# A selective scan laid out as 32 channels times 4 states, in a block with attention, feed-forward and routed low-rank layers

## What is computed

```python
dt = softplus(x_dbc[..., :R] @ dt_w + dt_b)
Bm, Cm = x_dbc[..., R:R + N], x_dbc[..., R + N:]          # N = 16 states
def step(h, inp):                                          # over the 512 tokens
    h = exp(dtt[..., None] * A) * h + (xt * dtt)[..., None] * Bt[:, None, :]
    y = einsum('bn,bdn->bd', Ct, h)                        # sum over the states
    return h, y
y = (y + x_c * D_param) * silu(z)
ssm_out = y @ ssm_out_w
```

## Time and profile before

| | |
|---|---|
| median of the runs | 5182.9 us (5181.59 to 5184.66, 3 runs) |
| span of the profiled execution | 5180.5 us |
| mean granted TensorE clock | 0.992 |
| PE busy | 4966.1 us, 96% |
| DVE busy | 4756.7 us, 92% |
| POOL busy | 4631.1 us, 89% |
| ACT busy | 4017.9 us, 78% |
| DMA | 812.29 MB, 157 GB/s |

### The profile page before, as it was taken

How to read it: one execution, slowest core, us unless ns; L and a number is a source line. 1 busy time by engine, 2 the same in 40 slices (tenths; PEclk the granted TensorE clock), 3 DMA queues, 4 the chain that set the end, 5 groups by cost and what they waited for, 6 DMA issues and landing times.

```text
span 5180.5 us, 94636 instructions
## 1 busy us (share of the span) xinstructions
PE 4966.1 (96%) x32312; PEld 3448.9 (67%) x32312; DVE 4756.7 (92%) x7342; ACT 4017.9 (78%) x6417; POOL 4631.1 (89%) x2933
## 2 busy tenths in 40 slices
PE   5899999999999999999999999999999999999998
PEld 2566666667666667666676666676666676666766
DVE  5999999999999999999999999999999999999985
ACT  4787887877877877877878878778778778787774
POOL 5899999999999999999999999999999999999984
PEclk7999999999999999999999999999999999999999
DMA  5455555555555555555555555555555545555552
GB/s 155 155 156 153 157 166 160 162 157 152 163 166 161 162 155 151 171 166 159 154 153 159 168 162 161 155 153 162 164 164 157 156 152 168 162 164 153 155 153 68
DMA packets 522032, 812.29 MB, mean 157 GB/s; under 512 B 80992, under 2 KB 227848, under 8 KB 521552
## 3 DMA queue, kind: packets, MB, share of 16 engines
q1 hardware_dynamic: 516784, 805.96, 51.2%
q10 hardware_dynamic: 4768, 0.28, 0.1%
HBM read 716.57 MB, written 88.38 MB: 155 GB/s over the span
## 4 chain that ended last, share of the span: by engine, by line
PE 72%; DVE 10%; issue 8%; POOL 5%; DMA 3%; SPq 1%; ACT 1%; DVEq 0%; POOLq 0%; ACTq 0%
PE pY L1083 12%; PE pM L1232 8%; PE pM L1241 8%; PE pM L1125 4%; PE pM L1219 4%; PE pM L1159 4%; PE pM L1172 4%; DVE pD L1466 4%; PE pM L1092 4%; PE pM L1105 3%; PE pM L1192 3%; POOL state L631 2%; PE pM L1133 2%; PE pM L1216 2%; PE pM L1140 2%
## 5 line engine op out<-in xcount | busy, mean ns | idle before, releaser
L631 POOL TENSOR_TENSOR state<-scan_in,bc 128x1024 f32<-128x1024 f32 x1024 | 2406.5, 2363 | 148.6 <-PE pY L1083 136.8
L788 ACT ACTIVATE pD<-scan_in,A 128x512 f32<-128x512 f32 x2048 | 1404.3, 690 | 400.8 <-DVE state L1474 315.3
L1466 DVE TENSOR_TENSOR_SCAN pD<-pD,state 128x512 f32<-128x512 f32 x1280 | 1545.1, 1219 | 68.9 <-ACT pD L788 67.6
L1083 PE MATMUL pY<-ident,state 128*128 128x128 f32 x8192 | 1152.6, 275 | 33.6 <-POOL state L619 26.6
L619 POOL TENSOR_TENSOR state<-state,bc 128x512 f32<-128x512 f32 x768 | 969.9, 1274 | 153.8 <-DVE state L1466 153.7
L1083 PEld LDWEIGHTS pY<-ident,state 128*128 128x128 f32 x8192 | 907.4, 142 | 269.2 <-issue 107.9
L1514 DVE TENSOR_REDUCE mx<-pM 128x1 f32<-128x512 f32 (+3 forms) x1408 | 859.9, 630 | 156.9 <-PE pM L1174 149.3
L1466 DVE TENSOR_TENSOR_SCAN state<-pD,state 128x512 f32<-128x512 f32 x768 | 916.3, 1210 | 57.3 <-ACT pD L788 57.2
L889 ACT ACTIVATE region<-pM 128x512 f32<-128x512 f32 (+1 forms) x1408 | 741.7, 559 | 179.6 <-PE pM L1194 157.0
L1474 DVE TENSOR_TENSOR state<-pD,bc 128x512 f32<-128x512 f32 x1280 | 862.0, 680 | 11.0
L1172 PE MATMUL pM<-region 96*128 96x512 bf16 (+3 forms) x2048 | 521.1, 301 | 25.8 <-DVE region L1531 11.1
(11 more groups left out here) (215 smaller groups left out, 8123.9 us busy)
## 6 DMA issues: line engine op xcount, KB each, us to landing
bc<-bc_d SPq DMA_DIRECT2D x2048, 256.0 KB, 3.9
region<-qk_d SPq DMA_DIRECT2D x640, 128.0 KB, 3.6
qk_d<-qkp SPq DMA_DIRECT2D x64, 384.0 KB, 3.4
qk_d<-ht SPq DMA_DIRECT2D x64, 384.0 KB, 5.1
xt<-in_x_dram SPq DMA_DIRECT2D x32, 512.0 KB, 5.4
hres_d<-xt SPq DMA_DIRECT2D x32, 512.0 KB, 4.4
region<-qk_d SPq DMA_DIRECT2D x256, 64.0 KB, 3.1
x<-hres_d SPq DMA_DIRECT2D x32, 512.0 KB, 5.2
```

The source lines that it names most:

```text
L631: nc.gpsimd.tensor_tensor(state[:, at_:at_ + JP], us[:, parity(b), k // N * JP:(k // N + 1) * JP, :], bc[:, k % BC_SLOTS, 0, :].unsqueeze( ...
L788: act.activation(pD[DECAY_BANK[e]][:], dts[:, parity(b), j], ACT.Exp, scale=A[:, j, n:n + 1]).then_inc(a_ok.sem, 1)
L1083: ins = pe.matmul(y_part(t, e % JP), state[:, e % RING, t * P:(t + 1) * P], ident[:], is_transpose=True, start=False, stop=(e % PASS >= PA ...
L1466: v.tensor_tensor_scan(h if e in POOL_C else decay, decay, h, 0.0, ALU.mult, ALU.add)\
```

## The change

The scans are laid out anew. A tile of 128 partitions now holds 32 channels times 4 states. There are 16 blocks of 32 channels; a pair of blocks and a group of 4 states is one unit, so there are again 32 units of two scans.

- dt and u are written to DRAM (`dtu_d`, two stores a turn), and read back 16 times a turn so that each row of 32 channels lands on four groups of partitions (`rep`, two slots). B and C need 8 loads a turn in place of 64, and stay for the whole turn.
- Every scan writes to `state` in SBUF. The C multiply is one operation of 128 x 1024 per unit, in place, on DVE for 20 units and on POOL for 12 (`k % 8` in 2, 5, 7).
- The states are added by PE: for each scan one product of the constant `sel` (128 x 32) with 512 columns of `state`, into the 32 rows of `pY` that belong to the block. The result has channels on the partitions, so `yt` (PE and ACT) is gone; `z` is computed with channels on the partitions too. The `D_param` term is a product with a diagonal matrix, so `ud` is gone.
- dt and u have one copy, `dtu`, where there were two. `nrm`, `ax`, `axT` and `gT` lie in it.
- All five orders and the bank places are new.

```diff
-UNITS = N * J // JP
+HALVES = J // JP
+CH = 32
+REP = P // CH
+SG = N // REP
+BLOCKS = DI // CH
+PAIRS = BLOCKS // JP
+UNITS = PAIRS * SG
 SCANS = UNITS * JP
-PASSES = J // JP
-PASS = SCANS // PASSES
+PASS = UNITS // J
 RING = 8
-BC_SLOTS = 4
-POOL_C = [e for e in range(SCANS) if e // JP % 4 == 3 or e % (4 * JP) == 2 * JP - 1]
+SLOTS = 2
+POOL_C = [k for k in range(UNITS) if k % 8 in (2, 5, 7)]
...
-        scan_in = sb("scan_in", [P, 2, 2, J, L])
-        dts, us = scan_in[:, :, 0], scan_in[:, :, 1]
+        dtu = sb("dtu", [P, J, 2, L])
+        dts, us = dtu[:, :, 0], dtu[:, :, 1]
+        rep = sb("rep", [P, SLOTS, JP, 2, L])
-        bc = sb("bc", [P, BC_SLOTS, 2, L])
+        bc = sb("bc", [P, 2, SG, L])
...
+            def spread(b, c):
+                if c % (PAIRS // HALVES) == 0:
+                    b.wait(sp, dtu_out[c * HALVES // PAIRS])
...
+                for i in range(JP):
+                    first = (c * JP + i) * CH
+                    src = dtu_d[b.index, first:first + CH].rearrange("d a t -> d (a t)")
+                    sp.dma_start(rep[:, c % SLOTS, i].rearrange("p a t -> p (a t)"),
+                                 src.unsqueeze(0).broadcast_to([REP, CH, 2 * L])).then_inc(rep_in[c % SLOTS].sem, 16)
...
+            def times_c(b, k):
+                at_, g = k * JP % RING, k % SG
+                b.wait(pool, s_ok, (k + 1) * JP)
+                b.wait(pool, bc_in[1][g])
+                nc.gpsimd.tensor_tensor(state[:, at_:at_ + JP], state[:, at_:at_ + JP],
+                                        bc[:, 1, g, :].unsqueeze(1).broadcast_to([P, JP, L]), ALU.mult).then_inc(pp_ok.sem, 1)
...
-                nc.gpsimd.tensor_tensor(state[:, at_:at_ + JP], us[:, parity(b), k // N * JP:(k // N + 1) * JP, :],
-                                        bc[:, k % BC_SLOTS, 0, :].unsqueeze(1).broadcast_to([P, JP, L]),
-                                        ALU.mult).then_inc(b_ok.sem, 1)
+                b.wait(pool, bc_in[0][g])
+                b.wait(pool, *rep_landed(c))
+                nc.gpsimd.tensor_tensor(state[:, at_:at_ + JP], rep[:, c % SLOTS, :, 1, :],
+                                        bc[:, 0, g, :].unsqueeze(1).broadcast_to([P, JP, L]), ALU.mult).then_inc(b_ok.sem, 1)
...
-                    b.wait(act, *decay_read_after(e - 1 - scanned))
+                    b.wait(act, s_ok, e + 1 - DECAYS)
...
-            def add(b, e):
-                b.wait(pe, *product_after(e))
-                for t in range(TB):
-                    ins = pe.matmul(y_part(t, e % JP), state[:, e % RING, t * P:(t + 1) * P],
-                                    ident[:], is_transpose=True, start=False,
-                                    stop=(e % PASS >= PASS - JP), skip_group_check=True)
+            def add(b, k):
+                j = k // PASS
+                b.wait(pe, *product_after(k))
+                for i in range(JP):
+                    rows = slice((k // SG % 2 * JP + i) * CH, (k // SG % 2 * JP + i + 1) * CH)
+                    ins = pe.matmul(pY[j % len(pY)][rows], sel[:], state[:, k * JP % RING + i], start=False,
+                                    stop=(k % SG == SG - 1), skip_group_check=True)
...
-                decay, h = pD[DECAY_BANK[e]][:], state[:, e % RING]
-                v.tensor_tensor_scan(h if e in POOL_C else decay, decay, h, 0.0, ALU.mult, ALU.add)\
-                 .then_inc(s_ok.sem, 1)
+                h = state[:, e % RING]
+                v.tensor_tensor_scan(h, pD[e % DECAYS][:], h, 0.0, ALU.mult, ALU.add).then_inc(s_ok.sem, 1)
...
-                v.tensor_tensor(state[:, e % RING], pD[DECAY_BANK[e]][:], bc[:, slot, 1, :], ALU.mult)\
-                 .then_inc(p_ok.sem, 1)
+            def times_c(b, k):
+                at_, g = k * JP % RING, k % SG
+                b.wait(dve, s_ok, (k + 1) * JP)
+                b.wait(dve, bc_in[1][g])
+                v.tensor_tensor(state[:, at_:at_ + JP], state[:, at_:at_ + JP],
+                                bc[:, 1, g, :].unsqueeze(1).broadcast_to([P, JP, L]), ALU.mult).then_inc(p_ok.sem, 1)
...
     "SP": """
+        qk3 xp -rp7 +load ld0 bb0 du0 bb1 -mt3 rp0 ld2 bb2 bb3 cc0 rp1 cc1 cc2 cc3 du1 ld1 mt0 rp2 rp3 +l1a -xr rp4
+        mt1 +qk0 rp5 x1p +qk1 rp6 ld3 -put +qk2 mt2
     """,
     "POOL": """
+        -fill27 -fill28 u0 -fill29 -pc26 u1 +l0s -fill30 -fill31 -pc29 fill0 fill1 -pc31 fill2 +l0a fill3 +l0b fill4
...
```

More of the change, by code:

```diff
@@ L462, in _ @@
                          d["lora_A"][:, k * P:(k + 1) * P, :].rearrange("e p r -> p e r"), w_late)
+            with nc.allow_non_contiguous_dma(reason="state indices go to partitions, once"):
+                for m in range(REP):
+                    for g in range(SG):
+                        n = g * REP + m
+                        load(A[m * CH:(m + 1) * CH, :, g:g + 1],
+                             d["A_log"][:, n:n + 1].rearrange("(c d) o -> d c o", d=CH), a_in)
+            assert n_loads.pop(a_in.name) == REP * SG
             assert n_loads == {"w_first": FIRST_LOADS, "w_loaded": N_LOADS - ACT_LOADS, "w_late": LATE_LOADS}, n_loads
@@ new lines, in step @@
+            def step(name, b):
+                if name[:2] in ("bb", "cc"):
+                    bc_rows(b, int(name[0] == "c"), int(name[2:]))
+                elif name[:2] == "rp":
+                    spread(b, int(name[2:]))
+                elif name[:2] == "du":
+                    h = int(name[2])
+                    b.wait(sp, u_ok, h + 1)
+                    rows = slice(h * JP * P, (h + 1) * JP * P)
+                    sp.dma_start(dtu_d[b.index, rows].rearrange("(j p) a t -> p j a t", p=P), dtu[:, h * JP:(h + 1) * JP])\
+                      .then_inc(dtu_out[h].sem, 16)
@@ L567, in _ @@
                 sp.wait_ge(qk_out[n].sem, 32 * B)
-            sp.wait_ge(bc_out.sem, 16 * PASSES * B)
+            sp.wait_ge(bc_out.sem, 16 * B)
+            for h in range(HALVES):
+                sp.wait_ge(dtu_out[h].sem, 16 * B)
         @block.gpsimd
@@ L801, in step @@
                 elif name == "l2a":
-                    normalise(b, 2, nrm(b), x1, n2)
+                    if not is_last(b):
+                        for h in range(HALVES):
+                            b.next().wait(act, dtu_out[h])
+                    normalise(b, 2, nrm, x1, n2)
                 elif name == "l3a":
-                    normalise(b, 3, nrm(b), xr, n3)
-                elif name == "ud":
-                    b.wait(act, u_ok)
-                    for j in range(J):
-                        act.activation(xc[:, j], xc[:, j], ACT.Copy, scale=D_par[:, j:j + 1]).then_inc(xd_ok.sem, 1)
+                    normalise(b, 3, nrm, xr, n3)
                 elif name[:2] == "xt":
@@ L1459, in _ @@
             dve.wait_ge(w_loaded, 16 * N_LOADS)
+            for j in range(J):
+                link(v.tensor_scalar(diag[:, j], ident[:], D_par[:, j:j + 1], None, ALU.mult))
+            assert count[0] == DIAG_READY
             def scan(b, e):
@@ L1664 @@
              + [(1, [0, 1]), (1, [2, 3]), (0, [0, 1, 2, 3])])
-N_LOADS = 24
+N_LOADS = 23
 ACT_LOADS = 17
```

364 lines of the change are left out of this document (162 added, 202 removed).

## The result

The changed kernel takes 7047.6 us (median of 4 runs, 7031.1 to 7057.9) against 5183.5 for the kernel before, a ratio of 1.359 with a 95% interval of 1.357 to 1.362. The sign came as forecast, the size did not: the forecast was 5700 us, in a range that ended at 5960.

What follows compares the result with a forecast made beforehand. It took PE to bound the kernel before, at 96% busy, with DVE and POOL close behind. After the change, contention makes a turn 173.2 us: 330.5 + 31 x 173.2 = 5700 us, range 5170 to 5960.

Steps and rivals of the forecast that it cites:

- the contention: DVE's two-SBUF multiplies and POOL's operations hold each other up: POOL 24.6 us, DVE 20 us more a turn.
- POOL and DVE were to be busy 95% or more: Sign in the profile after the change: waits from contention count as busy, with PE about 85%.
- where I put 1.0: DVE's mean wait per two-SBUF multiply for the rest of a running POOL operation: 1.0 us, 20 us a turn.
- my 0.96: PE's new adds: 0.96 us for each pair of products running side by side, 30.7 us a turn.
- the rival of pairs in series: PE's pairs of adds don't run side by side: 177.2 us a turn, 5820 us; chance 0.08.
- Store and load land in some 4 us each for 256 KB: Chain dt, u, store, spread load, fill: covered by POOL's other operations, nothing; without that cover up to 15 us a turn.
- Adding DVE's idle time of today, 9.4, gives 174: Turn from DVE's 164.7 us or POOL's 166.2 plus idle time: 174 or 173, taken as 173.2 us.
- with the orders planned for it: The single copy of dt and u ties the feed-forward between neighbouring batches' steps; costed at nothing.
- Sum: 152.9 - 40.2 + 34.3 = 147.0 us: PE's work per turn: 152.9 us, minus removed transposes, plus new adds and skip products, gives 147.0 us.
- the 330.5 us outside the turns: Time at the start and in the last batch, outside the 31 turns: 330.5 us, kept unchanged in the sum.
- 3.5 us a turn either way around 173.2: Spread within the main case: DVE's wait at 0.7 to 1.3 us gives 5590 to 5830 us.
- The rival "convoy": Ring of four units, store and reload, single copy on top of contention: 7 us more a turn, 5920 us; chance 0.10.

Runs made afterwards that it cites:

- e2: Changed kernel with DVE's C multiply replaced by a reduction of like length reading one SBUF tensor; narrow loads stay: 7064 us (1.363).
- e3: Changed kernel with both edits: loads with 32 channels outermost, and DVE's C multiply replaced by a reduction on one SBUF tensor: 6295 us (1.215).
- e1: Changed kernel with partitions laid out as 4 x channel + state, so that all loads have 32 channels outermost: 6518 us (1.258).
- e8: Kernel before with the source of its 32 loads of C rows a turn given outermost size 4 for 128, same bytes: 5808 us (1.121).
- e17: e14 with the change's own lists and bank places, each multiply split into halves behind its two scans: 6692 us (1.291).
- e14: e7 (16-engine loads, DVE's C multiplies reading PSUM, nothing left out) with lists and banks rearranged by a search: 5494 us (1.060).
- e13: e3 with only the five engines' lists and the banks rearranged by a search: 5912 us (1.140).
- e15: e1 with the lists of e13, the multiply on two SBUF tensors, nothing left out: 6367 us (1.228).
- e16: The changed kernel with the lists of e13 and nothing else, loads still narrow: 7977 us (1.539).
- e4: Kernel before with all scans written to `state` and DVE's 40 C multiplies reading two SBUF tensors: 6353 us (1.226).
- e18: e14 with each of PE's adds multiplying 128 of the 512 columns: 5491 us (1.060).
- e9: e3 with the state ring at 8 units instead of 4, other weights read to make room: 6303 us.
- e10: e3 with the reloads reading weight rows in place of stored dt and u, not waiting for the store: 6304 us.
- e7: Changed kernel with 16-engine loads, orders and banks of the kernel before, DVE's scans and multiplies in PSUM, nothing left out: 6488 us (1.252).

## Why the prediction was wrong

Right were the sign and two mechanisms, and the sign in part by luck: the term called decisive, the contention, was worth nothing in the changed kernel as it stands (e2), and much of the loss came from terms that the prediction put at nothing. POOL and DVE were to be busy 95% or more; they are at 71 and 73.

The multiply of two SBUF tensors and POOL's operations do hold each other up, both ways. With the multiply on one tensor (e3) the fills last 2396 ns at most; with two (e1) they go up to 3449, and the multiply up to 3412 where 1190 is its least. The Trainium skill, SBUF — State Buffer, Who interferes with whom, states that such a pair contends, and these rows agree. Sizes, e1 against e3: DVE's multiply 1.966 against 1.200 us, that is 0.77 of waiting where I put 1.0; all of POOL's busy time 5048.5 - 4580.6 = 468 us, 14.6 a turn, where I put 24.6; DVE's 14.7 where I put 20. The adds themselves were nearly right too: in e3 one pair's first record is followed by the next product after 3001.03 - 3000.04 = 0.99 us at the full clock, for my 0.96, so the rival of pairs in series falls:

```profile
3000.04 1.05 PE L1088 MATMUL pY<-state,sel 128*32 128x512 f32 x4
3001.03 0.39 PE L1176 MATMUL pM<-region 96*128 96x512 bf16 x1
```

The steps that failed:

1. **"Store and load land in some 4 us each for 256 KB, at worst four times that; ... so I cost it at nothing in a turn."** I read the landing time of a load whose outermost size was 128 and gave it to loads where it is 4. Measured: 530 us in this kernel (e1), 623 us for half the loads of B and C in the kernel before (e8). I also called the transfers lighter, 12 MB a turn for 16; bytes weren't what counted.
2. **"Adding DVE's idle time of today, 9.4, gives 174; adding to POOL's 166.2 some 7 of its 12.7 gives 173."** These idle times belong to the old lists, and I carried them over to five new ones; the single copy and the banks I put at nothing "with the orders planned for it". In e1, where the narrow loads are out of the way, the even stretch from 300 to 6100 us has DVE idle for 37 us of a turn of 197.9 and POOL for 41, where my sum had 9.4 and 7. PE, whose 3.6 us the rivals carry over, idles 25. That the lists can do this is shown in the PSUM form: 1198 us between e17 and e14, of them 461 through the clock. In the change's own form they can't be given one size: new lists are worth 383 us without the multiply (e3 to e13), 151 with it (e1 to e15), and lose 929 with the narrow loads (e16).
3. **The contention as a sum of busy times.** In e4 DVE's multiplies are 40 x 0.96 = 38 us a turn longer; the turn went from 156.45 to (6040.9 - 70.3) / 31 = 192.6, 36 us. So where DVE has little slack the sum of busy times holds. In the changed kernel the same term is worth 0 (e2), 223 (e3 against e1) or 455 us (e13 against e15), by what else binds. The term can't be priced without the lists.
4. **"Sum: 152.9 - 40.2 + 34.3 = 147.0 us" for PE.** PE's work did not fall. In e14, whose even stretch from 170 to 5250 us has a granted clock of 0.99, PE is busy 4947.99 / 5080 x 166.02 = 161.7 us a turn. The adds take 1084.0 / 32 = 33.9 us for my 30.7 and the skip 4.4 for 3.6. Most of the rest isn't in any group: the groups' busy times add up to 87 us more than before, but PE's busy time, in which overlapping groups count once, is 281 us more (5247.0 against 4966.1). So I took whole groups off a sum in which neighbours overlap. Why they overlap less now no run shows, and e18 shows that less PE work alone would not have made e14 faster.

Two smaller terms: the 330.5 us outside the turns are 7056.1 - 31 x 214.82 = 397 in the changed kernel, and 3.5 us a turn either way around 173.2 reach 5810 us at the top, not 5830.

The parts don't add up, as no part binds alone. From e1 to e14 it is 1024 us, by two edits: the PSUM form and lists made for it. The lists of e13 alone bring 151 (e15), the PSUM form alone loses 174 (e17). A cause for that loss is not shown; a likely one is that ACT's decays wait for DVE's multiplies too (522 us for L1484 in e17), so that DVE's scans wait 388 us for their decays, where they wait 284 in e1.

The rival "convoy", to which I gave 0.10, named store, reload and ring at 7 us a turn. Its ring and its chain are refuted as causes, each alone and in e3's lists (e9, e10); the single copy of dt and u, which it named too, was never taken away. What it had right is that a wait is passed on from engine to engine.

**Still open** is what holds e14 at 311 us over the kernel before, and how much of the change's own loss lies in the single copy of dt and u. It isn't PE's adds alone (e18). In e18 the chain is spread over everything,

```profile
PE 23%; DVE 18%; ACT 16%; issue 15%; POOL 15%; DMA 10%; SPq 3%; DVEq 0%; POOLq 0%; ACTq 0%
```

DVE and POOL are 88 and 83% busy, and ACT's decays wait 378 us for DVE's multiplies in PSUM. That could be lists that are still not the best, the two decay banks or the single copy; none was tried. No version measured here beats the kernel before.

## What to carry to other kernels

Look at the outermost size of both sides of every load that a change rewrites, before its bytes: 4 in place of 128 for half of them cost 12% in a kernel whose loads had been hidden (e8). In a kernel of in-order lists, idle time in the profile is a property of the lists and not of the work: when the lists are new, price them as an unknown of their own, with a bound on the slow side far wider than the old idle time. Do not take a group's busy time off an engine's total as if its neighbours did not overlap it. And test a suspected wait by taking it away: POOL's 1415 us of waits for PE were worth nothing.

## What the runs showed of the hardware

- At a DMA share of 0.25, a load with 4 outermost under way, 84 GB/s are moved, and other transfers of the same queue suffer: x lands 19.3 us after its issue with such loads around (changed kernel), 8.2 without (e1).
- A DVE multiply of 128 x 512 on two SBUF tensors beside a busy POOL takes 656 to 2872 ns, 1638 in the mean (e4); one of 128 x 1024 1966 (e1) or 2138 (e15). POOL's fills go up to 3432 ns in the changed kernel and 3449 in e1. DVE loses more than POOL in e4 (38 us a turn against 9); in e1 both lose the same (14.7 against 14.6).
- The adds of two units next to each other overlap when they write different pairs of strips, here in different banks of `pY` too (`add7 add8`): eight records in 1.40 us, where two units on the same strips (`add4 add5`) take 1.91. Both are from e3, at a granted clock of 1.00:

```profile
3006.94 1.91 PE L1088 MATMUL pY<-state,sel 128*32 128x512 f32 x8
3024.45 1.40 PE L1088 MATMUL pY<-state,sel 128*32 128x512 f32 x8
```

- TensorE's granted clock falls behind its own waits (from 1.00 to 0.50 in an idle stretch of 6.8 us of e7), and longer products cost 461 us beside 734 us of added waits (e17 against e14).
